# Routing weights of a mixture-of-experts feed-forward: a second buffer, and a new order of the stores, read-backs and matrix loads

## The chip, the cores and the metric

The kernel runs on one core of a Trainium2 chip. The metric is the device time of one launch, in microseconds (us). The engines are TensorE (PE), VectorE (DVE), ScalarE (ACT), GpSimd (POOL) and SyncE (SP), which here only issues transfers (DMAs).

## The reference

Four blocks are computed one after the other on x, of 4 batches by 512 tokens by 256 features, each as x = x + block(layernorm(x)): a cross-attention with an MLP, a feed-forward with 8 experts of which 2 are taken, a cross-attention with 16 heads, and last the feed-forward that matters here:

```python
probs = softmax(xf @ router_w + router_b)            # 64 experts
tw, ti = top_k(probs, 8)
tw = tw / sum(tw)
for e in range(64):                                  # routed experts, H = 64
    h = silu(xf @ w1[e] + b1[e]) @ w2[e] + b2[e]
    routed += where(ti == e, tw, 0).sum(-1) * h
shared = sum over 2 of silu(xf @ sw1 + sb1) @ sw2 + sb2   # HS = 512
return routed + shared
```

All of it is in float32.

## The kernel before

**Groups and units.** The last feed-forward (the code whose names begin with `d_`) does every expert for every token, and multiplies the hidden values by a weight that is zero where the expert was not chosen. The hidden width is cut into 10 groups of 512: groups 0 and 1 are the two shared experts (`GS = 2`), groups 2 to 9 hold 8 routed experts each (`GD = 10`). A unit u is one group g = u // 4 with one batch b = u % 4 of 512 tokens, so there are 40 units. Every matmul is done as three (`split_matmul`, L67 to L69), on the high and low parts of both operands.

**One unit.** PE makes four hidden tiles (`hidden(u)`: 24 matmuls of 512 columns). ACT applies silu to each (L1906), into the single buffer `d_hf`. In a routed group DVE multiplies each by the weights broadcast over partitions, `d_wb[b % 2]` (L1988). POOL rounds each to the high part (L873), DVE subtracts that for the low part (L878). PE then multiplies by the second matrix (`second(u)`: 48 matmuls of 256 columns) and DVE adds the result to X (L1978, `add_second(u)`).

**The order by hand.** PE's order is hidden(u + 1), second(u), and then the router's small steps. second(u) waits for the low parts of unit u and for add_second(u - 1), because it writes the same PSUM banks. DVE's order in unit u is: multiply by the weights (from unit 8 on), the four low parts, add_second(u - 1), the router's steps, and in the second unit of a group the split of the next group's matrices (L844, L847), which waits for ACT's copy (L831) and POOL's (L838); those wait for the load.

**The router.** The logits of batch b are made at the end of unit 1 + b, turned by PE in unit 2 + b, DVE takes their maximum (L1941) in unit 3 + b and ACT the exponentials. In unit 4 + b DVE runs `weights(b)`: from a reciprocal (L1948) to the eight greatest (L1956, L1961) and the normalised weights of 4 x 128 tokens by 64 experts, written to `d_w` (L1966, L1971). In unit 5 + b, after second(5 + b), PE turns `d_w` (`turn_weights(b)`, L1861), and ACT copies the result to `d_wT[b]` (L1899) at the end of its unit 6 + b. There is one `d_w`, so at L1965 `weights(b)` waits for turn_weights(b - 1) before L1966.

**SP's queue.** SP loads a group's matrices (`weights(g)`, L1772 and L1773, 512 KB each) once the split of group g - 1 is done, stores `d_wT[b]` to DRAM (L1786), and reads it back broadcast over partitions (`by_token(g, b, r)`, L1780, two DMAs of 512 KB each). It takes them strictly in the order written: groups 1 and 2, then store 0, read 0, store 1, read 1, store 2, store 3, then the load of group 3, read 2, read 3, the load of group 4 and so on. `d_wb` has two buffers, so a read r waits for the multiplication of unit r - 2 (counted from unit 8).

Of the kernel before, what the change touches and what calls it, by code (L numbers as in the profile page):

```python
# [12 lines left out]
ALU = mybir.AluOpType  # L13
AX = mybir.AxisListType

P = 128
B, S, D = 4, 512, 256
S2 = 1601
KD = D // P
QT = S // P  # L20
# [11 lines left out]
E1, H1 = 64, 64  # L32
# [39 lines left out]
def build_program(nc, x, ctxT, ctx, mask, cols, rows, l0_wq, l0_wkT, l0_wv, l0_w1, l0_w2, gate_wT,  # L72
                  mlp1, mlp2, mlp1_bT, mlp2_b, l1_wp, router_w, l1_w1, l1_w2, l1_b2, out):
    with ExitStack() as ctx_all:
# [147 lines left out]
        d_nm = sb("d_nm", [P, NT])  # L222
        d_sm = sb("d_sm", [P, NT])
        d_rsm = sb("d_rsm", [P, NT])
        d_w = sb("d_w", [P, QT, E1])
        d_wT = [sb(f"d_wT{b}", [E1 + ES, 512]) for b in range(B)]
        d_b2 = sb("d_b2", [E1 + ES, D])
        stD.close()
# [1537 lines left out]
        def d_sync(sp):  # L1766
            sp.dma_start(d_rw_raw[:, :, :], router_w.rearrange("(k p) e -> p k e", p=P)).then_inc(DR["w_in"], 16)
            sp.dma_start(d_b2[:, :], l1_b2).then_inc(DR["w_in"], 16)

            def weights(g):  # L1770
                sp.wait_ge(DM["w_lo"], g * 2)
                sp.dma_start(memD["w1r"][:, :, :], l1_w1[g].rearrange("(k p) n -> p k n", p=P)).then_inc(DM["w_in"], 16)  # L1772
                sp.dma_start(memD["w2r"][:, :, :], l1_w2[g].rearrange("(k p) n -> p k n", p=P)).then_inc(DM["w_in"], 16)  # L1773

            def by_token(g, b, r):

                wait_past(sp, DM["mul"], (r - 1) * 4)
                for s in range(2):
                    src = wscratch[(g - GS) * 8:(g - GS) * 8 + 8, b * S:(b + 1) * S].rearrange("(m s) t -> s m t", s=2)[s]
                    sp.dma_start(d_wb[b % 2][s * H1:(s + 1) * H1, :, :],  # L1780
                                 src.unsqueeze(0).to_broadcast([H1, 4, S])).then_inc(DM[f"wb_in{b % 2}"], 16)
            weights(1)
            weights(2)
            for b in range(B):
                sp.wait_ge(DR["wt_out"], (B + b) + 1)
                sp.dma_start(wscratch[0:E1, b * S:(b + 1) * S], d_wT[b][0:E1, :]).then_inc(DR[f"stored{b % 2}"], 16)  # L1786
                if b < 2:
                    sp.wait_ge(DR[f"stored{b % 2}"], 16)
                    by_token(GS, b, b)
            for g in range(GS, GD):  # L1790
                if g + 1 < GD:
                    weights(g + 1)
                for b in range(B):
                    if g == GS and b < 2:
                        continue
                    if g == GS:
                        sp.wait_ge(DR[f"stored{b % 2}"], 32)
                    by_token(g, b, (g - GS) * B + b)


# [4 lines left out]
        def d_pe(pe):  # L1805
            def hidden(u):
                g, b = u // B, u % B
                if b == 0:
                    pe.wait_ge(DM["w_lo"], g * 2 + 2)
                if g == 0:  # L1810
                    pe.wait_ge(LN["lo"], (3 * B + b) * 2 + 2)
                for m in range(4):
                    wait_past(pe, DM["act"], (u - 1) * 4 + m + 1)
                    for k in range(KD):
                        last = split_matmul(pe, PS[:, m, :], [w[:, k, m * P:(m + 1) * P] for w in memD["w1"][g % 2]],
                                            [ZT[:, b, h, k, :] for h in range(2)], k == 0, k == KD - 1)
                    last.then_inc(DM["h"], 1)

            def second(u):
                g, b = u // B, u % B  # L1820
                pe.wait_ge(DM["h_lo"], u * 4 + 4)
                wait_past(pe, x_done[3], u * 2)
                if g == GD - 1:
                    pe.wait_ge(DR["one"], B)
                    pe.wait_ge(DR["wt_out"], B + b + 1)
                    pe.wait_ge(DR["w_in"], 64)
                for i in range(QT):
                    o = PS[:, 4 + i // 2, (i % 2) * D:(i % 2 + 1) * D]
                    for k in range(4):
                        last = split_matmul(pe, o, [h[:, k, i * P:(i + 1) * P] for h in memD["h"][b % 2]],  # L1830
                                            [w[:, k, :] for w in memD["w2"][g % 2]], k == 0, k == 3 and g < GD - 1)
                    if g == GD - 1:
                        last = pe.matmul(o, d_wT[b][:, i * P:(i + 1) * P], d_b2[:, :], start=False, stop=True)  # L1833
                last.then_inc(DM["y"], 1)

            def logits(b):
                if b == 0:
                    pe.wait_ge(LN["lo"], 2 * B * 4)
                    pe.wait_ge(DR["w_lo"], 2)
                    pe.wait_ge(DR["w_in"], 64)  # L1840
                else:
                    pe.wait_ge(DR["lt_out"], B + b)
                for k in range(KD):
                    last = split_matmul(pe, PS[0:E1, 6, :], [w[:, k, :] for w in d_rw],
                                        [ZT[:, b, h, k, :] for h in range(2)], k == 0, k == KD - 1)
                last.then_inc(DR["lt"], 1)

            def turn_logits(b):
                pe.wait_ge(DR["lt_out"], B + b + 1)
                wait_past(pe, DR["exp"], b * QT)  # L1850
                for i in range(QT):
                    last = pe.transpose(d_turned(b)[:, i * E1:(i + 1) * E1], d_lt[b % 2][:, i * P:(i + 1) * P],
                                        ident[0:E1, 0:E1])
                last.then_inc(DR["lg"], 1)

            def turn_weights(b):
                pe.wait_ge(DR["w"], b * QT + QT)
                pe.wait_ge(DR["lt_out"], 2 * B)
                wait_past(pe, DR["wt_out"], B + b if b else 0)
                for i in range(QT):  # L1860
                    last = pe.transpose(PS[0:E1, 6, i * P:(i + 1) * P], d_w[:, i, :], ident[:, :])  # L1861
                last.then_inc(DR["wt"], 1)

            hidden(0)
            for u in range(DU):
                if u + 1 < DU:
                    hidden(u + 1)
                second(u)
                if u == 0:
                    for j in range(2):  # L1870
                        ln_turn(pe, 3, B - 1, j, 6 + j)
                if 2 <= u < 2 + B:
                    turn_logits(u - 2)
                if 1 <= u < 1 + B:
                    logits(u - 1)
                if 5 <= u < 5 + B:
                    turn_weights(u - 5)
# [58 lines left out]
        def d_dve(dve):  # L1936
# [7 lines left out]
            def weights(b):  # L1944
                ts = slice(b * QT, (b + 1) * QT)
                own = b * (3 * QT + 3)
                dve.wait_ge(DR["exp"], b * QT + QT)
                dve.reciprocal(d_rsm[:, ts], d_sm[:, ts]).then_inc(DR["own"], 1)  # L1948
                dve.wait_ge(DR["own"], own + 1)
                for i in range(QT):  # L1950
                    n = b * QT + i
                    dve.tensor_scalar(d_pr[:, n, :], d_pr[:, n, :], d_rsm[:, n:n + 1], None,
                                      ALU.mult).then_inc(DR["own"], 1)
                dve.wait_ge(DR["own"], own + QT + 1)
                for n in range(b * QT, b * QT + QT):
                    dve.max(d_top[:, n, :], d_pr[:, n, :]).then_inc(DR["own"], 1)  # L1956
                dve.wait_ge(DR["own"], own + 2 * QT + 1)
                dve.tensor_reduce(d_ts[:, ts], d_top[:, ts, :], AX.X, ALU.add).then_inc(DR["own"], 1)
                for i in range(QT):
                    n = b * QT + i  # L1960
                    dve.match_replace(d_mr[:, i, :], d_top[:, n, :], d_pr[:, n, :], -1.0).then_inc(DR["own"], 1)  # L1961
                dve.wait_ge(DR["own"], own + 2 * QT + 2)
                dve.reciprocal(d_rts[:, ts], d_ts[:, ts]).then_inc(DR["own"], 1)
                dve.wait_ge(DR["own"], own + 3 * QT + 3)
                wait_past(dve, DR["wt"], B + b if b else 0)  # L1965
                dve.scalar_tensor_tensor(d_w[:, :, :], d_mr[:, :, :], -1.0, d_pr[:, ts, :], ALU.is_equal,  # L1966
                                         ALU.mult).then_inc(DR["sel"], 1)
                dve.wait_ge(DR["sel"], b + 1)
                for i in range(QT):
                    n = b * QT + i  # L1970
                    dve.tensor_scalar(d_w[:, i, :], d_w[:, i, :], d_rts[:, n:n + 1], None, ALU.mult).then_inc(DR["w"], 1)  # L1971

            def add_second(u):
                b = u % B
# [992 lines left out]
```

## Time and profile before

| | |
|---|---|
| median of 3 runs | 1607.34 us (1606.03 to 1607.35) |
| the profiled execution | 1607.42 us, of which the span from first to last instruction is 1605.7 us |
| PE busy | 1517.9 us, 95% of the span |
| DVE busy | 1020.8 us, 64% |
| ACT busy | 705.4 us, 44% |
| last feed-forward | begins at 1114.9 us, 491 us to the end |
| mean granted TensorE clock | 0.982 of full speed |

Busy PE is an upper view: matmuls are pipelined. How long the engine works for a unit is better read from the distance between the starts of the same step in two units. Times inside the profile are counted from the span's start. Where a row gives a bracket at its end, it says how long the engine had been idle before it, and what released it.

### The profile page before, as it was taken

Reading aid. Unit: us, or ns where it says so; the run is one execution under the profiler, and the core shown is the slowest. Engines: PE = TensorE matmul, PEld = TensorE weight load, DVE = VectorE, ACT = ScalarE, POOL = GpSimd, SP = SyncE. Lnnn points to the kernel's source line nnn. Section 1 sums busy time; section 2 is a strip of 40 time slices with the busy share of each in tenths; the row PEclk is TensorE's granted clock in tenths of the full one; section 3 lists DMA queues with packets and bytes.
Section 4 is the critical chain, followed back from the end, with each engine's and each line's share of the span. In section 5 each row is a group of like instructions: output and inputs, shape, how many; then the busy total and the mean of one; then the engine's idle time right before and its main releaser. Section 6 shows DMA issues by size and latency. Waiting matters only on the chain.

```text
span 1605.7 us, 25045 instructions
## 1 busy us (share of the span) xinstructions
PE 1517.9 (95%) x8850; PEld 1180.6 (74%) x8850; DVE 1020.8 (64%) x2406; ACT 705.4 (44%) x1506; POOL 320.4 (20%) x346
## 2 busy tenths in 40 slices
PE   4999999996999989899999999998998899999998
PEld 3888888885566566666666666675888899999997
DVE  5566464455666767776666676775556667767664
ACT  2232232232655456566667666675343222222221
POOL 2202000225064242200000000010222232323221
PEclk9999999998999999999999999999999999999999
DMA  8431110412354110000000000001003856554432
GB/s 266 164 103 55 48 62 0 159 53 79 122 189 148 53 54 27 30 15 1 14 18 21 11 1 27 1 2 31 27 1 65 174 116 126 113 128 118 94 95 63
DMA packets 78179, 115.54 MB, mean 72 GB/s; under 512 B 7447, under 2 KB 51813, under 8 KB 77797
## 3 DMA queue, kind: packets, MB, share of 16 engines
q1 hardware_dynamic: 74981, 105.50, 23.6%
q0 software_dynamic: 3072, 8.39, 1.7%
q8 instruction: 75, 1.23, 0.3%
q14 instruction: 51, 0.42, 0.1%
HBM read 95.00 MB, written 18.87 MB: 71 GB/s over the span
## 4 chain that ended last, share of the span: by engine, by line
PE 55%; DVE 4%; issue 3%; ACT 2%; DMA 1%; POOL 0%; SPq 0%; DVEq 0%; ACTq 0%; POOLq 0%
PE PS L67 11%; PE PS L68 11%; PE PS L69 11%; PE PS L2524 7%; PE PS L2536 6%; PE PS L2512 5%; PE PS L2551 3%; ACT c_pr L2620 1%; DMA d_wb<-wscratch 1%; DVE c_sm L2729 0%; DVE c_c L2704 0%; PE PS L1833 0%; DVE c_pr L2738 0%; DVE X L1060 0%; DVE d_h L878 0%
## 5 line engine op out<-in xcount | busy, mean ns | idle before, releaser
L1906 ACT ACTIVATE d_hf<-PS,C 128x512 f32<-128x512 f32 x160 | 108.5, 690 | 269.7 <-PE PS L69 254.9
L2629 ACT ACTIVATE c_pt<-PS 100x512 f32<-100x512 f32 x256 | 139.1, 595 | 142.8 <-PE PS L2524 142.5
L67 PE MATMUL PS<-d_w,d_h 128*128 128x256 f32 x640 | 186.0, 291 | 12.1 <-DVE X L1978 10.6
L873 POOL CAST d_h<-d_hf 128x512 fp32r<-128x512 f32 x160 | 128.9, 819 | 312.9 <-DVE d_hf L1988 247.9
L68 PE MATMUL PS<-d_w,d_h 128*128 128x256 f32 x640 | 183.4, 287 | 0.0
L69 PE MATMUL PS<-d_w,d_h 128*128 128x256 f32 x640 | 183.4, 287 | 0.0
L2620 ACT ACTIVATE c_pr<-c_sm,c_mn 128x400 f32<-128x400 f32 x256 | 158.4, 626 | 28.1 <-DVE c_mn L2729 28.1
L2729 DVE CUSTOM_DVE_ANT_0 c_sm<-PS,c_mw 128x400 f32<-128x400 f32 x256 | 136.2, 570 | 27.6 <-PE PS L2512 22.5
L2524 PE MATMUL PS<-ident,c_pr 128*100 128x128 f32 x1024 | 139.4, 279 | 0.0
L878 DVE TENSOR_TENSOR d_h<-d_hf,d_h 128x512 fp32r<-128x512 f32 x160 | 129.1, 863 | 12.9 <-POOL d_h L873 12.9
L341 POOL TENSOR_TENSOR rs<-ve,halfneg 128x4 f32<-128x4 f32 x12 | 12.9, 1073 | 621.2 <-DVE ve L336 585.4
L67 PEld LDWEIGHTS PS<-d_w,d_h 128*128 128x128 f32 x640 | 125.2, 196 | 15.4 <-issue 13.6
L1988 DVE TENSOR_TENSOR d_hf<-d_hf,d_wb 128x512 f32<-128x512 f32 x128 | 90.9, 722 | 67.4 <-ACT d_hf L1906 64.7
L2524 PEld LDWEIGHTS PS<-ident,c_pr 128*100 128x100 f32 x1024 | 107.1, 129 | 35.1 <-issue 29.4
L67 PE MATMUL PS<-ZT,d_w 128*128 128x512 f32 x320 | 126.6, 396 | 1.9 <-issue 1.9
L68 PEld LDWEIGHTS PS<-d_w,d_h 128*128 128x128 f32 x640 | 125.2, 196 | 1.7
L68 PE MATMUL PS<-ZT,d_w 128*128 128x512 f32 x320 | 125.4, 392 | 0.0
L69 PE MATMUL PS<-ZT,d_w 128*128 128x512 f32 x320 | 125.2, 391 | 0.0
L69 PEld LDWEIGHTS PS<-d_w,d_h 128*128 128x128 f32 x640 | 125.1, 195 | 0.0
L2536 PE MATMUL PS<-c_pt,c_v 100*64 100x512 f32 x512 | 124.0, 605 | 0.0
L2512 PEld LDWEIGHTS PS<-c_k,c_q 64*128 64x128 f32 x768 | 62.1, 186 | 78.7 <-issue 70.4
L2512 PE MATMUL PS<-c_k,c_q 64*128 64x400 f32 x768 | 105.1, 379 | 5.2 <-DVE c_mn L2729 5.2
(296 smaller groups left out, 3071.7 us busy)
## 6 DMA issues: line engine op xcount, KB each, us to landing
d_wb<-wscratch SPq DMA_DIRECT2D x64, 512.0 KB, 7.8
a_cT<-ctxT SPq DMA_DIRECT2D x4, 1601.0 KB, 6.5
a_nat<-ctx SPq DMA_DIRECT2D x4, 1536.0 KB
zs<-e_zero SPq DMA_DIRECT2D x2, 2944.0 KB, 17.9
ys<-e_y SPq DMA_DIRECT2D x46, 128.0 KB, 1.7
e_z<-zs SPq DMA_DIRECT2D x10, 512.0 KB, 4.3
d_w1r<-l_w SPq DMA_DIRECT2D x10, 512.0 KB, 4.3
d_w2r<-l_w SPq DMA_DIRECT2D x10, 512.0 KB, 5.7
```

Source lines behind the costliest of these rows:

```text
L67: pe.matmul(out, w[0], x[0], start=first, stop=False)
L68: pe.matmul(out, w[0], x[1], start=False, stop=False)
L69: return pe.matmul(out, w[1], x[0], start=False, stop=last)
L873: i = eng.tensor_copy(mem["h"][b % 2][0][:, m, :], mem["hf"][:, m, :])
L878: eng.tensor_tensor(mem["h"][b % 2][1][:, m, :], mem["hf"][:, m, :], mem["h"][b % 2][0][:, m, :].bitcast(F32), ALU.subtract).then_inc(F["h ...
L1906: act.activation(memD["hf"][:, m, :], PS[:, m, :], ACT.Silu, bias=C[:, b1 + g * 4 + m:b1 + g * 4 + m + 1]).then_inc(DM["act"], 1)
L2512: last = pe.matmul(PS[:, BS + h, 0:WIN], c_q[u % 2][a][hs, i * P:(i + 1) * P], c_k[u % 2][c][hs, :], start=n == 0, stop=n == 2)
L2524: last = pe.transpose(PS[0:KW, BT + h, t * P:(t + 1) * P], c_pr[s % 3][h][:, t * KW:(t + 1) * KW], ident[:, :])
L2536: last = pe.matmul(PS[h * DH:(h + 1) * DH, BU, :], c_v[ph % 2][0:KW, t, p * P + h * DH:p * P + (h + 1) * DH], c_pt[u % 2][0:KW, h, t, :], ...
L2620: act.activation(c_pr[s % 3][h][:, :], c_sm[h][:, :], ACT.Exp, bias=c_mn[:, s % 4, h:h + 1], scale=-1.0, accum_out=c_l[:, s % 4, h:h + 1]) ...
L2629: act.activation(c_pt[u % 2][0:KW, h, :, i * P:(i + 1) * P], PS[0:KW, BT + h, :].rearrange("p (t q) -> p t q", q=P), ACT.Copy).then_inc(F[ ...
L2729: dve.tensor_tensor_reduce(c_sm[h][:, :], PS[:, BS + h, 0:WIN], c_mw[:, b * QT + i, :], 1.0, BIG, ALU.add, ALU.min, c_mn[:, s % 4, h:h + 1 ...
```

## The change

`d_w` gets two buffers, used in turn by the batches. `weights(b)` then waits only for turn_weights(b - 2). On SP, each batch's store is followed at once by the wait for it and its read-back, and the load of group 3 is issued between store 1 and its read. The load of group 4 comes after read 3.

```diff
-        d_w = sb("d_w", [P, QT, E1])
+        d_w = sb("d_w", [P, 2, QT, E1])
...
                 sp.wait_ge(DR["wt_out"], (B + b) + 1)
                 sp.dma_start(wscratch[0:E1, b * S:(b + 1) * S], d_wT[b][0:E1, :]).then_inc(DR[f"stored{b % 2}"], 16)
-                if b < 2:
-                    sp.wait_ge(DR[f"stored{b % 2}"], 16)
-                    by_token(GS, b, b)
-            for g in range(GS, GD):
+                if b == 1:
+                    weights(GS + 1)
+                sp.wait_ge(DR[f"stored{b % 2}"], 16 * (b // 2 + 1))
+                by_token(GS, b, b)
+            for g in range(GS + 1, GD):
                 if g + 1 < GD:
                     weights(g + 1)
                 for b in range(B):
-                    if g == GS and b < 2:
-                        continue
-                    if g == GS:
-                        sp.wait_ge(DR[f"stored{b % 2}"], 32)
                     by_token(g, b, (g - GS) * B + b)
...
-                    last = pe.transpose(PS[0:E1, 6, i * P:(i + 1) * P], d_w[:, i, :], ident[:, :])
+                    last = pe.transpose(PS[0:E1, 6, i * P:(i + 1) * P], d_w[:, b % 2, i, :], ident[:, :])
...
-                wait_past(dve, DR["wt"], B + b if b else 0)
-                dve.scalar_tensor_tensor(d_w[:, :, :], d_mr[:, :, :], -1.0, d_pr[:, ts, :], ALU.is_equal,
+                wait_past(dve, DR["wt"], B + b - 1 if b >= 2 else 0)
+                dve.scalar_tensor_tensor(d_w[:, b % 2, :, :], d_mr[:, :, :], -1.0, d_pr[:, ts, :], ALU.is_equal,
                                          ALU.mult).then_inc(DR["sel"], 1)
...
-                    dve.tensor_scalar(d_w[:, i, :], d_w[:, i, :], d_rts[:, n:n + 1], None, ALU.mult).then_inc(DR["w"], 1)
+                    dve.tensor_scalar(d_w[:, b % 2, i, :], d_w[:, b % 2, i, :], d_rts[:, n:n + 1], None, ALU.mult).then_inc(DR["w"], 1)
```

## Rows read from the trace of the kernel before

**Rows 1.** The page: span, and busy time of PE over the whole kernel.
```profile
span 1605.7 us, 25045 instructions
...
PE 1517.9 (95%) x8850; PEld 1180.6 (74%) x8850; DVE 1020.8 (64%) x2406; ACT 705.4 (44%) x1506; POOL 320.4 (20%) x346
```
**Rows 2.** Busy time by stretch, cut where PE starts units; the first row names the columns.
```profile
core 0: us, PE busy (x) PEld busy (x) DVE busy (x) ACT busy (x) POOL busy (x), PEclk, DMA share, GB/s
1198.13:1211.54 13.41, 11.53 (x76) 10.27 (x73) 9.86 (x33) 5.46 (x14) 1.79 (x4) 1.00 0.05 11
1211.54:1223.22 11.68, 11.68 (x78) 10.69 (x77) 7.25 (x30) 3.35 (x5) 0.56 (x1) 1.00 0.65 122
1223.22:1241.54 18.32, 14.54 (x78) 13.24 (x77) 14.94 (x23) 3.26 (x5) 8.86 (x8) 0.81 0.23 52
1241.54:1253.22 11.68, 11.68 (x78) 10.70 (x77) 3.23 (x4) 3.62 (x6) 1.04 (x1) 1.00 0.77 179
1253.22:1272.29 19.07, 14.09 (x75) 12.81 (x74) 14.65 (x19) 2.92 (x5) 8.11 (x8) 0.82 1.02 205
1272.29:1283.51 11.22, 11.22 (x75) 10.26 (x74) 6.88 (x10) 2.76 (x4) 2.85 (x4) 1.00 0.32 82
1296.00:1584.00 288.00, 288.00 (x1836) 262.87 (x1835) 194.63 (x266) 75.84 (x108) 87.54 (x107) 1.00 0.48 112
```
**Rows 3.** PE in order of time: first matmuls of second(6), second(8), second(10), idle in brackets.
```profile
1205.71 0.35 PE L67 MATMUL PS<-d_w,d_h 128*128 128x256 f32 x1 [1.88 <-DVE X L1978]
...
1233.09 0.55 PE L67 MATMUL PS<-d_w,d_h 128*128 128x256 f32 x1 [3.78 <-DVE X L1978]
...
1263.83 0.55 PE L67 MATMUL PS<-d_w,d_h 128*128 128x256 f32 x1 [4.98 <-DVE X L1978]
```
**Rows 4.** DVE in order of time: start, duration, line, idle before it.
```profile
1172.76 0.17 DVE L1948 RECIPROCAL d_rsm<-d_sm 128x4 f32<-128x4 f32 x1
...
1175.92 0.74 DVE L1971 TENSOR_SCALAR d_w<-d_w,d_rts 128x64 f32<-128x64 f32 x4
...
1198.48 0.42 DVE L1966 SCALAR_TENSOR_TENSOR d_w<-d_mr,d_pr 128x256 f32<-128x256 f32 x1 [9.93 <-PE PS L1861]
...
1223.92 0.43 DVE L1966 SCALAR_TENSOR_TENSOR d_w<-d_mr,d_pr 128x256 f32<-128x256 f32 x1 [4.29 <-PE PS L1861]
...
1231.67 1.27 DVE L1978 TENSOR_TENSOR X<-PS,X 128x512 f32<-128x512 f32 x2
...
1251.28 1.23 DVE L844 TENSOR_TENSOR d_w<-d_w1r,d_w 128x1024 fp32r<-128x1024 f32 x1 [8.26 <-ACT d_w L831]
...
1255.92 3.33 DVE L1988 TENSOR_TENSOR d_hf<-d_hf,d_wb 128x512 f32<-128x512 f32 x4 [2.28 <-DMA d_wb<-wscratch]
1259.17 3.31 DVE L878 TENSOR_TENSOR d_h<-d_hf,d_h 128x512 fp32r<-128x512 f32 x4
```
**Rows 5.** ACT in order of time: copy of the first turned weights, and group 3's first matrix.
```profile
1207.11 0.59 ACT L1899 ACTIVATE d_wT<-PS 64x512 f32<-64x512 f32 x1
...
1250.19 1.06 ACT L831 ACTIVATE d_w<-d_w1r 128x1024 fp32r<-128x1024 f32 x1 [7.42 <-DMA d_w2r<-l_w]
```
**Rows 6.** SP in order of time: issues, the stretch they span, and how many.
```profile
1210.03 1.29 SPq L1780 DMA_DIRECT2D d_wb<-wscratch  x2
1212.79 0.48 SPq L1786 DMA_DIRECT2D wscratch<-d_wT  x1
1220.42 1.23 SPq L1780 DMA_DIRECT2D d_wb<-wscratch  x2
1224.47 18.80 SPq L1786 DMA_DIRECT2D wscratch<-d_wT  x2
1243.65 0.37 SPq L1772 DMA_DIRECT2D d_w1r<-l_w  x1
1244.08 0.50 SPq L1773 DMA_DIRECT2D d_w2r<-l_w  x1
1244.69 2.66 SPq L1780 DMA_DIRECT2D d_wb<-wscratch  x4
```
**Rows 7.** Transfers by tile, issue to landing: first the stores of d_wT, then the reads into d_wb.
```profile
DMA to landing us min/median/max: 2.3/3.7/7.6
```
```profile
DMA to landing us min/median/max: 5.7/7.8/15.2
```

## The prediction

> **What bounds the kernel now.** The page first: PE is busy for 1517.9 of 1605.7 us, 95% [rows 1], so time can only come out of the few stretches in which PE stands, or from its clock. The change touches the last feed-forward alone, so I cut PE's time there at the starts of its units [rows 2]. From unit 11 on a unit takes 11.22 us (5.46 us of hidden, 5.76 of second), and the 288 us from 1296 to 1584 are PE busy without a gap at clock 1.00. Where turn_weights and the switch around it are in a unit, it takes 11.68 us, as units 7 and 9 show. The three others of this stretch are long: unit 6 with 13.41 us, unit 8 with 18.32, unit 10 with 19.07. The reader is to see two things in them: PE busy is short of the stretch, and the clock of the last two is 0.81 and 0.82. PE in order of time gives the idle parts: 1.88, 3.78 and 4.98 us, each ahead of a second(u), each ended by DVE's addition to X [rows 3].
>
> What holds DVE up is in its own rows [rows 4]. For stalls one and two it is L1966: weights(1) stood 9.93 us for turn_weights(0), and weights(3) 4.29 us for turn_weights(2). DVE is in order, so the split of group 2, the low parts and the addition come behind. After the second of these waits (1223.92) DVE works nearly without a pause up to the addition at 1231.67, and that takes another 1.3 us, so PE's banks come free only at 1232.9. For stall three it is SP: DVE waited 8.26 us for ACT's copy of group 3's matrix and then 2.28 us for read 2. ACT in turn had waited for the load, and ran at 1250.19 [rows 5]. SP had issued that load at 1243.65, behind store 3 (the last of the two stores in the row that begins at 1224.47), and read 2 behind it at 1244.69 [rows 6]. Yet the load needed only the split of group 2, done at about 1202 (1198.48 plus 0.42 + 0.74 for d_w and two operations of 1.2 us).
>
> **Part 1, the second buffer.** It adds no instruction and takes away the binding of weights(b) to turn_weights(b - 1). weights(b) may run as soon as its exponentials are there; it takes 3.9 us from its reciprocal to its last product (1172.76 to 1176.66, the case without a wait [rows 4]).
> - weights(1) ends at 1189.8 instead of 1199.7. The split of group 2 (two operations of 1.2 us) is over by 1193, low parts of unit 6 by 1196.5 (3.3 us with POOL beside it [rows 4]), both under second(5), which ends at 1197.4. The addition of unit 5 then ends at 1198.8, and second(6) can start at 1203.7, right behind hidden(7). Stall one is gone.
> - The addition's earlier end brings forward the maximum of batch 3, its exponentials and ACT's copy of the turned weights 0: from 1207.11 [rows 5] to about 1200.4. weights(2) starts at 1199.1 and ends at 1203; weights(3), behind add_second(6) at 1211, ends at 1214.9. Its remaining wait, for turn_weights(1), was met at 1209.8. In unit 8 four multiplications and four low parts (3.3 us each) end by about 1221, paced by ACT; the addition of unit 7 follows at 1222.5, and PE needs it at 1227. Stall two is gone with 4 us to spare.
>
> **Part 2, SP's order.** With PE dense from 1198.13, unit 6 ends at 1209.5 (13.41 less 2.08, below), unit 7 at 1221.1, unit 8 at 1232.8, unit 9 at 1244.5, unit 10 at 1255.7. The turned weights 1, 2 and 3 are copied 1 us behind the first three: 1210.5, 1222.3 and 1234. So:
> - Load of group 3: SP issues it behind store 1, at about 1211.1; its condition (split of group 2) has been met since 1193. It took 6.5 us in the trace (1243.65 to 1250.19 [rows 5, 6]) and is there at about 1218. ACT's copy then waits only for turned weights 3, so the split of group 3 ends by about 1237.4, not 1253.6. It is inside hidden(10).
> - Read 0 is issued at about 1203.9, needed from 1214.9, and lands at 1211.7 by the median of 7.8 us [rows 7].
> - Read 1: a store takes 2.3 to 7.6 us [rows 7], the longest being store 1, issued at 1212.79 while read 0 was under way, so that read 1 went out at 1220.42 [rows 6]. In the new order store 1 comes at 1210.6, when read 0 is nearly in. Read 1 goes out at 1214 to 1218 and lands between 1222 and 1229.2 (7.8 us by the median; 11.2 us as read 2 took behind a load of 1 MB, from 1244.69 to 1255.92 [rows 4, 6]). Second(9) starts at 1238.8; less 3.3, 3.3 and 1.3 us for multiplications, low parts and addition, DVE may start as late as 1230.9.
> - Read 2: turned weights at 1222.3, store by 1226 (at worst 1230), landing at 1234 (at worst 1241); the limit by the same sum is 1242.1 for second(10) at 1250. It is wanted at 1237.4, behind the split.
> - Read 3: copy at 1234.6, store by 1238.3 (worst 1242.2), landing at 1246.1 (worst 1253.4); limit 1253.3 for second(11) at 1261.2.
> - The wait on each store now keeps SP from what is behind it. Behind waits 2 and 3 stand store 3 and the load of group 4. The first is not ready before 1234, the second not wanted before unit 13. Cost nothing; without that cover it would be up to 7.6 us on the load, still five units early.
> - d_w takes 1 KB more of each partition. Nothing executes for it: nought.
>
> **The sum.** By stretch: unit 6, 13.41 - (11.68 - 0.35, no turn ahead of it) = 2.08 us; unit 8, 18.32 - 11.68 = 6.64 us; unit 10, 19.07 - 11.22 = 7.85 us. Together 16.57 us [rows 2]. Of it 10.64 us is idle time [rows 3] and 5.9 us matmuls at the lower clock: the clock was 1.00 in unit 6, whose gap was 1.88 us, and fell behind the gaps of 3.78 and 4.98 us. As the gaps go, I take both. The two parts bring 8.7 us (units 6 and 8) and 7.9 us (unit 10). Bounds of the clock's term: 0 and 5.9 us; the 288 us without a gap held 1.00, so I take 5.9. Bounds of the idle term: 10.64, and 5.66 if the third stall stays. After unit 11 the units cost what they do now, as PE is full there. 1607.42 - 16.6 = **1590.8 us**; the profiled execution is 0.08 us above the median shown, so against this the same.
>
> **Rivals.**
> 1. *The read-backs arrive late.* Reads 1 and 2 now share the DMA engines with the 1 MB load, and the time between copy and use of batch 3 is only 12 us. With the longest store and the longest read of the rows, 7.6 + 15.2 us from 1234.6, read 3 lands at 1257.4, 4.1 us after its limit; with the clock after such a gap (2.9 us, half of the 5.9) that is 7.0 us: 1597.8 us. For it: the 7.6 us of the store behind a read. Against: every median lands in time, with 3 to 8 us to spare, and the same pattern (1 MB load, then reads) recurs through 288 us without a gap. 8%. The Trainium skill, "DMA: Bandwidth & Descriptors", section "Queues, rings and completion order", says that a completion is posted by a DMA engine only after all its earlier writes. By that rule read 1 and store 2 report only after the load in front of them; the rows of store 1 agree (7.6 against 2.3 us). The time it would make is this rival's.
> 2. *The change does only half of what it says.* DVE stays the limit in unit 10, for instance because the split of group 3 waits for POOL or ACT in another way (ACT's copy stands behind turned weights 3 in its order), or SP's part alone is too late. Then 7.9 us of the sum stay: 1598.7 us. Against: in later groups the same order of split and units runs without a gap. 6%.
> 3. *Slower than before.* SP's strict order becomes a chain: store, wait, read, for four batches, with the load inside, each behind the last. It decides from where read 3 lands after 1253.3 + 16.6 - 2.9 = 1267.0, 32 us after its store is issued, where the longest pieces seen make 23 us. If each took twice its longest, read 3 would land 45.6 us behind the issue, at 1280.2, 26.9 us after its limit, and the time would be 1590.8 + 26.9 + 2.9 = 1620.6 us. 3%.
> 4. *No change*: the chain of rival 3 is late by just what the change saves, read 3 landing between about 1264 and 1270: 1604.4 to 1610.4 us. 3%.
>
> **The numbers.** My forecast has 80%. It is 1589.5 to 1593 by itself (repeats of the kernel before differ by 1.3 us; a first read late by a microsecond or two is hidden). Rivals 1 and 2 spread from there to 1599; the range goes to 1597, which takes in part of them. 0.2% is 3.2 us, about what a measurement of this kernel can tell from no change. Faster by more than that: 0.80 + 0.08 + 0.06 = 0.94; within: 0.03; slower: 0.03.
>
> **What would show it.** In the profile after: no idle PE ahead of second(6), second(8), second(10), and clock 1.00 in all of 1198 to 1256; the hidden of unit 12 starts at 1255.7, not 1272.29; L1966 without a wait; ACT's L831 for group 3 with no wait on a DMA, at about 1235; the load of group 3 issued at about 1211, read 3 at about 1238. I am wrong if a second(u) is ended by L1978 behind a DMA of d_wb (rival 1) or behind L844 (rival 2), or if the clock stays low without gaps.

## The result, and the profile after

The changed kernel takes 1590.73 us (median of 4 runs, 1588.84 to 1592.23), the kernel before 1607.34 us in the same comparison: a ratio of 0.990, 95% interval 0.9886 to 0.991, or 16.6 us less. The profiled execution took 1590.48 us. Predicted were 1590.8 us.

The page of the changed kernel, and who PE waited for from 1190 us to the end (engine, line, who was late: us in all, times, longest):

```profile
span 1588.7 us, 25044 instructions
...
PE 1511.5 (95%) x8850; PEld 1175.7 (74%) x8850; DVE 1023.2 (64%) x2406; ACT 706.4 (44%) x1506; POOL 321.0 (20%) x346
```
```profile
PE PS L67 <- issue: 1.4, 1, 1.4
```

PE has the same 8850 matmuls and is busy 6.4 us less: matmuls at the lower clock are longer, and those behind the three gaps are gone. Of the 6.4 us, 6.0 lie in the five units from hidden(7) on (57.55 us busy, before 63.52 by the sum of [rows 2]). From 1190 us on one wait of 1.4 us is left, ahead of the very last second step. The three waits for the addition to X [rows 3] are gone. Lines from L1786 on are numbered three lower than before.

The busy time by stretch, cut at the starts of the same units as [rows 2] (the columns are those of that group):

```profile
1197.79:1209.43 11.64, 11.64 (x79) 10.69 (x77) 8.48 (x32) 5.47 (x14) 3.23 (x4) 1.00 0.46 73
1209.43:1221.12 11.69, 11.69 (x80) 10.70 (x77) 11.01 (x35) 3.35 (x5) 4.81 (x4) 1.00 0.97 217
1221.12:1232.80 11.68, 11.68 (x80) 10.70 (x77) 7.72 (x11) 3.35 (x5) 4.30 (x5) 1.00 0.54 107
1232.80:1244.12 11.32, 11.32 (x75) 10.34 (x73) 9.89 (x12) 4.19 (x6) 4.06 (x4) 1.00 0.47 103
1244.12:1255.34 11.22, 11.22 (x74) 10.26 (x73) 6.88 (x10) 2.76 (x4) 2.86 (x4) 1.00 1.03 226
1255.34:1266.56 11.22, 11.22 (x74) 10.26 (x73) 6.88 (x10) 2.76 (x4) 2.86 (x4) 1.00 0.41 100
1280.00:1568.00 288.00, 288.00 (x1839) 262.95 (x1838) 194.06 (x265) 75.82 (x109) 88.19 (x108) 1.00 0.49 111
```

(Each of the first three stretches ends with a turning, where [rows 2] cut ahead of it; the fourth has none. Both sets begin at hidden(7) and reach hidden(12).) Every unit costs what PE needs for it, at clock 1.00. From the start of hidden(7) to the start of hidden(12) it is 57.55 us, where before it was 74.16: 16.61 us of the 17.0 us by which the span is shorter. The other 0.3 us lie ahead of hidden(7). This stretch is the measure of all that follows.

DVE in order of time:

```profile
1188.24 0.42 DVE L1963 SCALAR_TENSOR_TENSOR d_w<-d_mr,d_pr 128x256 f32<-128x256 f32 x1
...
1193.05 3.71 DVE L878 TENSOR_TENSOR d_h<-d_hf,d_h 128x512 fp32r<-128x512 f32 x4 [0.51 <-POOL d_h L873]
...
1213.19 0.42 DVE L1963 SCALAR_TENSOR_TENSOR d_w<-d_mr,d_pr 128x256 f32<-128x256 f32 x1
...
1220.96 1.29 DVE L1975 TENSOR_TENSOR X<-PS,X 128x512 f32<-128x512 f32 x2
...
1234.65 1.23 DVE L844 TENSOR_TENSOR d_w<-d_w1r,d_w 128x1024 fp32r<-128x1024 f32 x1 [0.72 <-ACT d_w L831]
...
1236.93 3.32 DVE L1985 TENSOR_TENSOR d_hf<-d_hf,d_wb 128x512 f32<-128x512 f32 x4
...
1246.50 0.69 DVE L1985 TENSOR_TENSOR d_hf<-d_hf,d_wb 128x512 f32<-128x512 f32 x1 [0.89 <-ACT d_hf L1903]
```

The product that writes `d_w` runs without a wait for batch 1 (1188.24, before 1198.48) and batch 3 (1213.19, before 1223.92) [rows 4]. Group 3's split begins at 1234.65, before 1251.28, and its wait is 0.72 us for ACT's copy, not 8.26. The multiplications of units 10 and 11 (the last two rows) wait for no transfer. ACT and SP:

```profile
1199.95 0.59 ACT L1896 ACTIVATE d_wT<-PS 64x512 f32<-64x512 f32 x1
...
1233.57 1.05 ACT L831 ACTIVATE d_w<-d_w1r 128x1024 fp32r<-128x1024 f32 x1
```
```profile
1202.88 1.29 SPq L1780 DMA_DIRECT2D d_wb<-wscratch  x2
1210.33 0.48 SPq L1786 DMA_DIRECT2D wscratch<-d_wT  x1
1210.87 0.58 SPq L1772 DMA_DIRECT2D d_w1r<-l_w  x1
...
1212.95 1.24 SPq L1780 DMA_DIRECT2D d_wb<-wscratch  x2
1222.02 0.48 SPq L1786 DMA_DIRECT2D wscratch<-d_wT  x1
1224.30 1.24 SPq L1780 DMA_DIRECT2D d_wb<-wscratch  x2
1233.70 0.48 SPq L1786 DMA_DIRECT2D wscratch<-d_wT  x1
1235.97 1.23 SPq L1780 DMA_DIRECT2D d_wb<-wscratch  x2
```

The load of group 3 goes out at 1210.87, before at 1243.65 [rows 6], and ACT's copy at 1233.57 waits no more for it. Each read follows its store by 2.3 to 2.6 us. The transfers by tile, from issue to landing, first the stores and then the reads, against [rows 7]:

```profile
DMA to landing us min/median/max: 2.3/2.3/2.6
```
```profile
DMA to landing us min/median/max: 5.5/7.8/14.6
```

### The profile page after: what moved, and what is told of

It is laid out like the page before. It is cut to its first block, busy times and chain, and to the rows that moved or that the text cites. A ratio compares the mean times of both kernels' runs of the same rounds, so it can differ in the third digit from the quotient of the medians.

```text
span 1588.7 us, 25044 instructions
## 1 busy us (share of the span) xinstructions
PE 1511.5 (95%) x8850; PEld 1175.7 (74%) x8850; DVE 1023.2 (64%) x2406; ACT 706.4 (44%) x1506; POOL 321.0 (20%) x346
## 3 DMA queue, kind: packets, MB, share of 16 engines
q0 software_dynamic: 3072, 8.39, 1.7%
## 4 chain that ended last, share of the span: by engine, by line
PE 58%; DVE 3%; ACT 2%; issue 1%; DVEq 0%; ACTq 0%
PE PS L67 12%; PE PS L68 12%; PE PS L69 12%; PE PS L2521 7%; PE PS L2533 6%; PE PS L2509 5%; PE PS L2548 3%; ACT c_pr L2617 1%; DVE c_sm L2726 1%; DVE c_pr L2735 0%; DVE c_c L2701 0%; PE PS L1830 0%; DVE X L1060 0%; DVE c_u L2739 0%; ACT c_pt L2626 0%
## 5 line engine op out<-in xcount | busy, mean ns | idle before, releaser
L67 PE MATMUL PS<-d_w,d_h 128*128 128x256 f32 x640 | 183.2, 286 | 1.4 <-issue 1.4
L68 PE MATMUL PS<-d_w,d_h 128*128 128x256 f32 x640 | 181.1, 283 | 0.0
L69 PE MATMUL PS<-d_w,d_h 128*128 128x256 f32 x640 | 181.1, 283 | 0.0
L67 PEld LDWEIGHTS PS<-d_w,d_h 128*128 128x128 f32 x640 | 122.6, 192 | 3.7 <-issue 1.8
L68 PEld LDWEIGHTS PS<-d_w,d_h 128*128 128x128 f32 x640 | 122.6, 192 | 1.9
L69 PEld LDWEIGHTS PS<-d_w,d_h 128*128 128x128 f32 x640 | 122.6, 192 | 0.0
```

Of the source, the lines that this page charges most:

```text
L67: pe.matmul(out, w[0], x[0], start=first, stop=False)
L68: pe.matmul(out, w[0], x[1], start=False, stop=False)
L69: return pe.matmul(out, w[1], x[0], start=False, stop=last)
```

## The experiments

When the experiments ran, the kernel before took 1637 to 1638 us. The extra 30 us lie ahead of hidden(7), which starts at 1226 to 1237 us in all of these profiles; kernels whose code is the same up to there differ in this start by 10 us, and single runs of one kernel by up to 8.5 us in all. So the stretch from hidden(7) to hidden(12), 57.55 us when PE is never idle, decides, and medians stand beside it.

| kernel | median us | ratio to before | stretch us | idle ahead of second(6), (8), (10) |
|---|---|---|---|---|
| before, first profile | 1607.34 | | 74.16 | 1.88, 3.78, 4.98 |
| before, again | 1635.77 (one run) | | 72.34 | 1.88, 3.78, 4.53 |
| changed, first profile | 1590.73 | 0.990 (0.9886 to 0.991) | 57.55 | none |
| changed, again | 1623.72 | 0.991 (0.988 to 0.994) | 57.55 | none |
| second buffer alone | 1627.42 | 0.994 (0.992 to 0.996) | 63.81 | 0, 0, 4.55 |
| SP's order alone | 1631.86 | 0.996 (0.995 to 0.9975) | 66.56 | 1.87, 3.77, 0 |
| changed, load of group 3 late | 1635.06 | 0.998 (0.997 to 0.999) | 70.00 | 0, 0, 2.28; and 6.63 ahead of hidden(11) |
| changed, reads 2 and 3 late | 1623.22 | 0.991 (0.989 to 0.9925) | 61.49 | 0, 0, 2.23 |

### The two kernels again

> The changed kernel itself, on the same chip and in the same job as the next ones. The stretch from the start of hidden(7) to the start of hidden(12) was 74.16 us before and 57.55 us after the change. Theory (it is PE-bound there, and the rest of the kernel does not change): 57.5 us again whatever the absolute time of the chip, and 16 to 17 us less than the kernel before in the same job. Rival (the gain came from the particular chip or run): a stretch that differs by microseconds, or a different gain.

> The kernel before once more, in the job of the next ones, where the absolute times are some 30 us above those of the first measurement. Theory: the same three gaps ahead of second(6), second(8) and second(10), 1.9, 3.8 and 4.5 to 5.0 us, so 67.7 to 68.2 us plus what the matmuls behind them lose to the clock: the clock's part was 5.4 us in the first profile, and 1.5 us for a single gap in the experiments so far, so the stretch is 72 to 74.2 us. Rival (the extra 30 us lie in this stretch): a longer one.

The changed kernel's stretch came out at 57.55 us again. Its gain did not: 14.5 us by the medians, where 16 to 17 were expected. The kernel before took 72.34 us, with the first two gaps as before and the third 0.45 us shorter:

```profile
PE PS L67 <- DVE X L1978: 10.2, 3, 4.5
PE PS L67 <- issue: 1.4, 1, 1.4
```

Most of the rest is clock. With 10.2 us of idle time, 72.34 - 57.55 - 10.2 leaves 4.6 us, of which second(8) takes 2.7 (8.43 us against 5.75) and second(10) 1.4 (7.13). In the first profile they took 2.7 each. The last 0.5 us, the same in both profiles, are not in these two steps: each hidden step ahead of a gap takes 0.16 us more than a dense one, its gap left out, and second(6) 0.08 us. So by the stretch the gain is 14.8 us here and 16.6 us there, with the same three gaps; the medians say the same (14.5 and 16.6 us), but their intervals overlap.

### The second buffer alone

```diff
-                if b == 1:
-                    weights(GS + 1)
...
+                if b < 2:
+                    sp.wait_ge(DR[f"stored{b % 2}"], 16)
+                    by_token(GS, b, b)
+            for g in range(GS, GD):
...
```

> The second buffer alone; SP's order is that of the kernel before. Theory (the two parts remove different stalls, and each gap over 3.7 us also costs 2.9 us of clock): no idle PE ahead of second(6) and second(8); ahead of second(10) the gap stays, because group 3's matrices are loaded only behind store 3 (issued at about 1235, landed 1241.5, split to 1245) and read 2 behind them (to 1247), so the addition ends at 1255 where PE could start at 1249.6: a gap of 5 us and 2.9 us of clock, 1598.7 us. Rival (the buffer does it all, the order of SP was only late because of the earlier stalls): 1591 us. Rival (the buffer brings nothing without the order): 1607 us.

The stretch is 63.81 us, 6.3 us above the changed kernel's, and the median 10.2 us below the kernel before's. Two of the three gaps are gone, and the third stands nearly as before. DVE in order of time:

```profile
1272.95 1.23 DVE L844 TENSOR_TENSOR d_w<-d_w1r,d_w 128x1024 fp32r<-128x1024 f32 x1 [8.39 <-ACT d_w L831]
...
1277.03 3.33 DVE L1988 TENSOR_TENSOR d_hf<-d_hf,d_wb 128x512 f32<-128x512 f32 x4 [1.72 <-DMA d_wb<-wscratch]
```

It waits 8.39 us for the copy of group 3's matrix and 1.72 us for read 2, as in [rows 4] (8.26 and 2.28). The rivals, in which the buffer does all or nothing, fall. The expected 8.0 us of leftover came out as 6.3: 4.55 instead of 5 us of idle, 1.55 instead of 2.9 us of clock.

### SP's order alone

The edit is the change's part in SP's queue put into the kernel before; `d_w` stays single, and so does its wait.

> SP's new order alone, with one d_w. Theory: the stalls ahead of second(6) (1.9 us) and second(8) (3.8 us and 2.9 us of clock) stay as in the kernel before, L1966 waits again for the turning of the batch before; the gap ahead of second(10) is gone. 1590.7 + 8.7 = 1599.4 us. Rival (SP's order brings all, since ACT and DVE catch up): 1591 us. Rival (the order brings nothing while the turned weights are late): 1607 us.

The stretch is 66.56 us, 9.0 us above the changed kernel's, where 8.7 were expected. That it is so near is in part luck: 2.9 us of clock were expected behind the second gap alone, and it was 1.5 us behind each of the two (second(6) took 7.30 us, second(8) 7.23). The first two gaps are those of the kernel before, the third is gone, and DVE waits for the turning as before:

```profile
1235.17 0.42 DVE L1963 SCALAR_TENSOR_TENSOR d_w<-d_mr,d_pr 128x256 f32<-128x256 f32 x1 [9.93 <-PE PS L1858]
...
1262.09 0.42 DVE L1963 SCALAR_TENSOR_TENSOR d_w<-d_mr,d_pr 128x256 f32<-128x256 f32 x1 [4.28 <-PE PS L1858]
```

Against the 72.34 us of the kernel before, the buffer alone brings 8.5 us and the order alone 5.8 us, together 14.3, and the two at once 14.8. In idle time they add up gap by gap: the buffer takes away the first two gaps, the order the third, and neither needs the other. The clock's share does not belong to a part in this way: it was 0.1 us in second(6) in both profiles of the kernel before and 1.5 us here, behind the same gap. Against the 74.16 us of the first profile the two parts would be 10.4 and 7.6 us, together 18.0, where the change brought 16.6.

### The order in its own two parts

```diff
-                if b == 1:
-                    weights(GS + 1)
                 sp.wait_ge(DR[f"stored{b % 2}"], 16 * (b // 2 + 1))
                 by_token(GS, b, b)
+            weights(GS + 1)
```

> The changed kernel with the load of group 3 behind read 3 instead of ahead of read 1; reads stay early. Theory (the load ahead carries part 2): issued at 1237.3 behind read 3, landed at about 1246 to 1248, split to 1250.5, then multiplications, low parts and addition (7.9 us) to 1258.4 where PE could start second(10) at 1249.6: gap 8.8 us and 2.9 us of clock, 1602.4 us. Rival (the early reads carry it): 1591 to 1593 us.

The stretch is 70.00 us, 12.5 us above the changed kernel's (11.7 expected): reads early without the load early is a loss. The way there was another than expected. ACT, in order of time:

```profile
1280.36 1.06 ACT L831 ACTIVATE d_w<-d_w1r 128x1024 fp32r<-128x1024 f32 x1 [15.56 <-DMA d_w2r<-l_w]
1281.33 2.41 ACT L1902 ACTIVATE d_hf<-PS,C 128x512 f32<-128x512 f32 x4
```

ACT stood 15.56 us for the load, and the silu of unit 10 is behind that copy in its order. PE makes hidden(11) into the same banks, so it stood for ACT first, and only 2.28 us were left for the addition:

```profile
1282.05 0.79 PE L67 MATMUL PS<-ZT,d_w 128*128 128x512 f32 x1 [6.63 <-ACT d_hf L1902]
...
1291.63 0.36 PE L67 MATMUL PS<-d_w,d_h 128*128 128x256 f32 x1 [2.28 <-DVE X L1974]
```

The two gaps make 8.9 us, and slow matmuls most of the rest: hidden(11) took 1.8 us more than a dense one, and second(10) 1.55 us (7.30 against 5.75).

With the second buffer in place, reads early and load late is worse (70.00) than the order of before (63.81): in that one the load was ahead of read 2, and here it is behind read 3. So the 12.5 us are the price of a load behind all four reads, where no other kernel here has it, and not what the early load brings.

```diff
                 if b == 1:
                     weights(GS + 1)
-                sp.wait_ge(DR[f"stored{b % 2}"], 16 * (b // 2 + 1))
-                by_token(GS, b, b)
+                if b < 2:
+                    sp.wait_ge(DR[f"stored{b % 2}"], 16)
+                    by_token(GS, b, b)
...
```

> The changed kernel with the load of group 3 early, but reads 2 and 3 only behind store 3, as before. Theory (the reads' order has slack to spare): read 2 is issued at 1236.3 instead of 1224.3, lands at 1244 to 1246 where the limit for second(10) is 1241.7: a gap of 2 to 4 us, with clock loss only if it is near 4, so 1593 to 1597 us. Rival (the load alone does it): 1590.7 us. Rival (the reads are worth as much as the load): 1598.7 us.

The stretch is 61.49 us, 3.9 us more, in the middle of what was expected: a gap of 2.23 us and 1.55 us of second(10) at the lower clock. That a gap so short costs clock was not expected. DVE:

```profile
1275.02 3.33 DVE L1990 TENSOR_TENSOR d_hf<-d_hf,d_wb 128x512 f32<-128x512 f32 x4 [7.06 <-DMA d_wb<-wscratch]
```

It stood 7.06 us for read 2, and only 2.23 of them reached PE. The medians (1623.22 and 1623.72) cannot tell this kernel from the changed one; the profile can.

The two experiments together say what the order's parts are worth beside the second buffer. From its 63.81 us, the early load alone brings 2.3 us (61.49), the early reads alone cost 6.2 us (70.00), and both bring 6.3 us (57.55). So neither carries the order's part by itself: the early reads bring 3.9 us, but only with the load ahead of them.

### How much room read 3 has

Both kernels add stores of the same values, each waited for, ahead of read 3 (three, and six in the other):

```diff
+                if b == 3:
+                    for k in range(3):
+                        sp.dma_start(wscratch[0:E1, b * S:(b + 1) * S], d_wT[b][0:E1, :]).then_inc(DR["stored1"], 16)
+                        sp.wait_ge(DR["stored1"], 32 + 16 * (k + 1))
                 by_token(GS, b, b)
```

> The changed kernel with three more stores of the same weights, each waited for, ahead of read 3 only. A store and its wait took 2.3 us, so read 3 is issued 6.9 us later than 1236.0 (in the times of the changed kernel's profile), at 1242.9, and lands at about 1250.7. Theory (read 3 has until 1252.9: second(11) starts at 1260.8, less 7.9 us of multiplications, low parts and addition): no gap, a stretch of 57.5 us to hidden(12) and no idle PE ahead of second(11). Rival (the read-backs have no slack, rival 1 of the prediction): a gap of up to 6.9 us.

> As before this one but six more stores: read 3 is issued 13.8 us later, at 1249.8, and lands at 1257.6, 4.7 us after the limit. Theory: one gap of 4 to 5 us ahead of second(11), and 1.5 to 2.9 us of clock behind it, 6 to 8 us in all. The load of group 4 is late by the same 13.8 us and costs nothing, as it is wanted only in unit 13. Rival (more slack than thought, because DVE and ACT can catch up): no gap. Rival (the delay goes through in full): 14 us.

These two kernels and the three of the next section ran once each (1618.84 and 1629.54 us; 1626.63, 1627.68 and 1638.31 us), so only their profiles are read. Three stores cost nothing: 57.56 us to hidden(12), and no idle PE ahead of second(11), which started at 1289.15. But it was close. DVE in order of time:

```profile
1281.22 3.33 DVE L1989 TENSOR_TENSOR d_hf<-d_hf,d_wb 128x512 f32<-128x512 f32 x4 [7.26 <-DMA d_wb<-wscratch]
1284.46 3.31 DVE L878 TENSOR_TENSOR d_h<-d_hf,d_h 128x512 fp32r<-128x512 f32 x4
1287.70 1.27 DVE L1979 TENSOR_TENSOR X<-PS,X 128x512 f32<-128x512 f32 x2
```

The addition ended at 1288.97, 0.2 us before PE wanted it. The multiplications began 55.1 us behind hidden(7), just where the expectation had put the last moment for them (1252.9 - 1197.8). DVE had stood 7.26 us for the read at no cost. With six stores the same wait reaches PE:

```profile
1289.66 3.32 DVE L1989 TENSOR_TENSOR d_hf<-d_hf,d_wb 128x512 f32<-128x512 f32 x4 [14.23 <-DMA d_wb<-wscratch]
```
```profile
1297.56 0.55 PE L67 MATMUL PS<-d_w,d_h 128*128 128x256 f32 x1 [6.76 <-DVE X L1979]
```

The gap was 6.76 us and second(11) took 8.06 us, so 9.1 us in all, above the expected 6 to 8. The read's price was too small: from the issue of the first of its two DMAs (1279.29) to the multiplication it took 10.4 us, not 7.8, and 10.1 us with three stores. 7.8 us is the median of one DMA. A read is two of them: in the changed kernel read 2, with nothing right behind it, landed 9.3 us after its first issue (1224.30 to 1233.60), and read 3, with the load of group 4 right behind it, after 10.0 us (1235.97 to 1245.93).

### What a gap costs in clock

Fills of a dead tile on DVE, ahead of add_second(19), put a gap of chosen length into an otherwise dense stretch:

```diff
+                if u == 20:
+                    dve.wait_ge(DR["sel"], B)
+                    for k in range(8):
+                        dve.wait_ge(DR["own"], B * (3 * QT + 3) + k)
+                        dve.memset(d_pr[:, :, :], 0.0).then_inc(DR["own"], 1)
```

> Seven fills instead of eight ahead of add_second(19). One fill with the wait on itself took 1.19 us, and eight gave a gap of 3.76 us and a second(20) of 7.31 us. Theory: a gap of 2.6 us; with the clock falling as after the gap of 2.23 us in the run with late reads, second(20) takes about 7.3 us. Rival (the clock falls only behind gaps of 3.7 us and more, as in the first profile, where 1.88 us cost nothing): 5.75 us.

> The changed kernel with eight fills of a dead tile (128 x 1024) on DVE in unit 20, ahead of add_second(19): about 1 us each by the 0.485 us of a fill of 512. DVE has 1.5 us idle there and PE needs the sum 4.2 us after it could be ready. Theory (a gap in PE costs its length and then matmuls at the lower clock): a gap of 2 to 3 us ahead of second(20), and 0 to 3 us more of second(20) (5.75 us at the full clock), by the clock of the rows. Rival (the clock's term belongs to the stretch, not to the gap): second(20) takes 5.75 us.

> Ten fills. Theory: a gap of 6.1 us, and second(20) takes between 7.3 and 8.5 us, the two values seen behind gaps. Rival (the clock's loss grows with the gap): more than 8.5 us.

PE's first matmul of second(20) with seven, eight and ten fills:

```profile
1396.38 0.36 PE L67 MATMUL PS<-d_w,d_h 128*128 128x256 f32 x1 [2.57 <-DVE X L1975]
```
```profile
1397.39 0.35 PE L67 MATMUL PS<-d_w,d_h 128*128 128x256 f32 x1 [3.76 <-DVE X L1975]
```
```profile
1406.85 0.55 PE L67 MATMUL PS<-d_w,d_h 128*128 128x256 f32 x1 [6.14 <-DVE X L1975]
```

The gap with eight was longer than the expected 2 to 3 us, because a fill with the wait on itself took 1.19 us, not 1. second(20) then took 7.32, 7.31 and 8.52 us, against 5.75 us at the full clock. So here too, where nothing else is changed, a gap ahead of one step cost its length and 1.6 to 2.8 us of slow matmuls behind it: the loss comes with the gap and not with the first routed units. It does not grow with the gap in proportion: 2.57 and 3.76 us cost the same, and the gap of 6.76 us above cost less (8.06) than this one of 6.14.

### The last gap

```diff
-                wait_past(pe, x_done[3], u * 2)
+                if u < DU - 1:
+                    wait_past(pe, x_done[3], u * 2)
+                else:
+                    pe.wait_ge(DM["act"], u * 4 + 4)
...
-                    o = PS[:, 4 + i // 2, (i % 2) * D:(i % 2 + 1) * D]
+                    o = PS[:, (4 if u < DU - 1 else 0) + i // 2, (i % 2) * D:(i % 2 + 1) * D]
```

(and the same banks in `add_second`)

> The changed kernel; the last unit's second step writes to the PSUM banks of the hidden tiles, which ACT has read by then, instead of the two that wait for the addition of the unit before. Theory (with the three gaps gone, the 1.4 us ahead of second(39) are the last idle time of PE in this feed-forward): no gap there, 1.3 us less than the changed kernel, which is below what a comparison of medians can tell on this chip; the profile decides. Rival (second(39) then waits for its low parts instead): the gap stays.

PE is not idle once between hidden(7) and the end of its work. From hidden(7) to the end of the span it is 389.2 us (1619.4 - 1230.16), in the changed kernel 391.0 us (1618.5 - 1227.52, and 390.9 in its first profile): 1.7 us less. The median was 1620.8 us, with a ratio of 0.989 (0.986 to 0.991) to the kernel before, where the changed kernel, compared on another occasion, had 0.991 (0.988 to 0.994). The intervals overlap, so that it beats the changed kernel is shown by the profile's stretch alone.

## Why the prediction was right

- **What bounds the kernel, and the sum by stretch.** It held to 0.1 us: 16.57 us from three long units, 16.61 us measured from hidden(7) to hidden(12). What made it work was to take the long units' excess over a PE-bound one, and then to show for each that nothing else becomes late. The last tenth is luck: the four runs of the changed kernel spread over 3.4 us, and by the second profile of the kernel before the same sum would have been 14.8 us.
- **Part 1.** The second buffer removes stalls one and two and nothing else, as the kernel with it alone showed. weights(1) ended at 1189.4 (forecast 1189.8), the first turned weights were copied at 1199.95 (1200.4).
- **Part 2.** The load went out at 1210.9 (1211.1), the split ended at 1237.0 (1237.4), and the third stall was gone. The forecast relied on both halves of the new order, and the kernel needs both: beside the second buffer the early load alone brings 2.3 of the 6.3 us, and the early reads alone cost 6.2 us.
- **The terms that were mis-sized.** The 5.9 us that were put down to the clock were right as a sum for the profile that they were read from, but 5.4 of them are slow second steps and 0.5 us the small extra around the gaps. Nor are they a constant: in the second profile of the kernel before they were 4.6 us, and so the third stall was worth less. By the 72.34 us of that profile the order brings 5.8 us, not 7.9, and the buffer 8.5, not 8.7. The read was taken as 7.8 us by the median of one DMA, and a whole read with a load behind it took 10.0 to 10.4 us; the "at worst" of 11.2 us was the nearer figure. The load of group 3 took 8.7 us (1210.87 to 1219.62), not 6.5, and ACT wanted it only at 1233.57. Stores went the other way: 2.3 to 2.6 us where up to 7.6 were allowed for, because store 1 is issued when read 0 has only 2.4 us to go (it landed at 1212.77), store 2 when read 1 has 0.7 us to go, and store 3 when no read is under way. For read 3 the two errors nearly cancel: it was issued at 1235.97, forecast 1238.3, and landed at 1245.93, forecast 1246.1. It had 7.2 us of room by the forecast, and 6.8 us of delay left 0.2.
- **Rival 1** (late read-backs) did not come about, but it was near: at three more stores the room was used up, at six it cost 9.1 us. The rule of the Trainium skill that it leaned on ("DMA: Bandwidth & Descriptors", "Queues, rings and completion order": a completion comes only after the DMA engine's earlier writes) fits the runs. In the kernel before, store 1 was issued while read 0 was under way, took 7.6 us, and landed at 1220.40, 0.3 us behind the read (1220.06). In the changed kernel it was issued later in the read, took 2.6 us, and landed 0.2 us behind it (1212.94 and 1212.77). Read 1 landed behind the load in front of it (1220.88 and 1219.62).
- **Rival 2** (half of the gain) did not come about. Its stall in unit 10 is what the second buffer alone leaves: 6.3 us, where the rival had 7.9. Nothing in the runs speaks for rivals 3 and 4.

## What to carry to other kernels

Where an engine is dense but for a few long units, take each long unit's excess over a dense one, trace the wait back to the first instruction that was late in its engine's order, and give every part of a change its own stall: here two independent ones, whose idle times add. Work out for each hidden transfer the last moment at which it may land, and test that limit by delaying it: in unit 11 a wait of 7.26 us on DVE was free and one of 14.23 us cost 9.1 us, while in unit 10, where DVE has a split to do first, one of 7.06 us cost 3.9 us. The length of a wait off the critical path does not tell its price. In a queue that one engine issues in order, what is needed by the longest chain (a load, its copy, its split) goes ahead of what is merely ready: with the load behind read 3 the kernel lost 12.5 us.

## What the runs showed of the hardware that had not been expected

- The clock's loss behind a gap of PE is not given by the gap's length. Gaps of 1.88 us cost next to nothing in two profiles, and 1.87 us cost 1.5 us in another (the second step behind it took 7.30 us instead of 5.83). Behind gaps of 2.23, 2.28 and 2.57 us it took 7.30, 7.30 and 7.32 us. Gaps of 3.76 to 3.78 us were followed by second steps of 7.31, 7.23, 8.45 and 8.43 us, gaps of 4.53 to 4.98 us by 7.13, 7.30 and 8.46, and gaps of 6.14 and 6.76 us by 8.52 and 8.06. Beside its length one gap cost between 0.1 and 2.8 us, at a granted clock of 0.50, which is 1.2 instead of 2.4 GHz. Why two gaps of one length cost differently was not tested.
- A store of 128 KB took 2.3 us when no read was under way. Where a read had longer to go than that, the store landed just behind it: stores 1 and 2 of the kernel before took 7.61 and 4.83 us and landed 0.3 and 0.2 us behind reads 0 and 1.
- The same kernel took 1607 us on one occasion and 1636 to 1638 us on others, with the last feed-forward alike to 0.01 us where PE was dense. The difference lies in earlier blocks, 27 of the 30 us between 443 and 517 us: PE was busy for 190.8 us of the 200 us from 400 to 600 us in the first profile of the kernel before, and for 176.9 us in the second (granted clock 0.98 and 0.92). Its cause was not looked for.
